# Idle TensorE multiplies constants before the second table and before the experts, and some register loads take bounds checks

## The reference

```python
x = x + gnn0(ln(x), src, dst, edge_weight, W, b)        # sum over 100000 edges of weighted rows, then @ W.T + b
x = x + ffn0(ln(x), wr, br, w1, b1, w2, b2)             # half of the rows chosen by a router, 256 -> 1024 -> 256
x = x + gnn1(ln(x), edge_weight1, weight, gate_weight, src, dst, edge_type_16)
#   all_msg = einsum('nf,rfo->rno', h, weight)          # 16 relations: the "second table"
#   msg = all_msg[rel, src] * norm * sigmoid(gate[rel, src]);  agg = segment_sum(msg, dst);  relu
x = x + ffn1(ln(x), Wg, bg, W1, b1, W2, b2)             # 8 experts, the top 2 of each row, 256 -> 1024 -> 256
```

## Time and profile before

| | |
|---|---|
| median of three executions | 4001.26 us (3999.29 to 4010.76) |
| span of the profiled execution, first to last instruction | 3402.6 us |
| median less span | 598.7 us |
| mean granted TensorE clock | 0.902 of full speed |
| TensorE busy | 2615.4 us, 77% of the span |
| GpSimd busy | 1869.7 us, 55% |
| VectorE busy | 1733.1 us, 51% |
| ScalarE busy | 723.6 us, 21% |

### The profile page before, as it was taken

One profiled execution on the slowest core, in us unless ns is written; L12 is line 12 of the kernel. 1 busy time (PEld: TensorE's weight loads), 2 busy tenths in 40 slices (PEclk: granted clock), 3 DMA queues, 4 the chain that ended last, 5 costly groups with the idle time before them and its releaser, 6 DMA issues. The chain is left out here.

```text
span 3402.6 us, 59974 instructions
## 1 busy us (share of the span) xinstructions
PE 2615.4 (77%) x14271; PEld 1921.6 (56%) x14272; DVE 1733.1 (51%) x5663; ACT 723.6 (21%) x1907; POOL 1869.7 (55%) x1915
## 2 busy tenths in 40 slices
PE   7688888887777799999655555564555389999997
PEld 6577777776665344444344444443444267767774
DVE  6455545454554655555355454544544544545553
ACT  4121111111110233333211010000000233333332
POOL 1777777777774000000377777777777245555554
PEclk9899999998999899999888888777777689999998
DMA  7333333333332444444545454555544623222232
GB/s 224 110 113 113 113 111 111 113 113 113 110 113 67 173 197 192 188 191 194 194 141 155 151 154 142 152 154 151 146 146 146 241 59 48 45 45 48 45 48 33
DMA packets 175589, 434.08 MB, mean 128 GB/s; under 512 B 41712, under 2 KB 103792, under 8 KB 169232
## 3 DMA queue, kind: packets, MB, share of 16 engines
q0 software_dynamic: 97072, 236.21, 26.9%
q1 hardware_dynamic: 57424, 183.78, 14.1%
q10 hardware_dynamic: 21008, 13.24, 1.3%
HBM read 275.05 MB, written 158.04 MB: 127 GB/s over the span
## 5 line engine op out<-in xcount | busy, mean ns | idle before, releaser
L776 POOL DMA_INDIRECT g_msg<-table,idx x1564 | 1517.3, 970 | 518.8 <-issue 476.5
L848 PE MATMUL psum<-g_msg,g_hot 128*128 x3328 | 967.4, 456 | 593.0 <-SPq L719 358.1
L848 PEld LDWEIGHTS psum<-g_msg,g_hot 128*128 128x128 f32 x3328 | 756.5, 233 | 789.5 <-issue 654.5
L796 DVE TENSOR_SCALAR g_hot<-iota,g_cols 128x128 f32<-128x128 f32 x1664 | 450.1, 364 | 31.9 <-DVE g_cols L793 30.5
L1908 POOL DMA_INDIRECT out<-ex_y,ex_to x112 | 206.0, 1839 | 253.9 <-DMA out<-ex_y,ex_to 165.3
L768 POOL MEMSET g_origin<- 128x256 f32 x1 | 0.3, 313 | 590.8 <-POOLq L1359 590.8
L1594 PE MATMUL psum<-wrel_halves,t_xhi 128*128 128x512 f16 x784 | 298.2, 380 | 1.7 <-DVE t_row L1475 1.7
L1595 PE MATMUL psum<-wrel_halves,t_xhi 128*128 128x512 f16 x784 | 298.1, 380 | 0.0
L1596 PE MATMUL psum<-wrel_halves,t_xlo 128*128 128x512 f16 x784 | 298.1, 380 | 0.0
L1475 DVE TENSOR_SCALAR t_row<-psum,t_gate 128x256 f32<-128x256 f32 x392 | 171.2, 479 | 233.7 <-PE psum L1596 231.7
L2074 PE MATMUL psum<-w,ex_ghi 128*128 x784 | 260.6, 382 | 6.7 <-DVE ex_y L1983 6.4
(11 more groups left out here) (353 smaller groups left out, 3231.7 us busy)
## 6 DMA issues: line engine op xcount, KB each, us to landing
table<-t_row SPq DMA_DIRECT2D x48, 2048.0 KB, 6.3
g_msg<-table,idx POOLq DMA_INDIRECT x1564
piece_stage<-in_w SPq DMA_DIRECT2D x32, 512.0 KB, 5.7
w_halves<-piece_halves SPq DMA_DIRECT2D x32, 512.0 KB, 3.4
w<-w_halves SPq DMA_DIRECT2D x8, 2048.0 KB, 22.6
rows<-sc_row ACTq DMA_DIRECT2D x50, 128.0 KB, 2.2
out<-acc ACTq DMA_DIRECT2D x49, 128.0 KB
table<-t_row SPq DMA_DIRECT2D x24, 256.0 KB, 2.5
```

Of the source, the lines that this page charges most:

```text
L776: pool.indirect_dma_start(out=msg[:, at:at + D], out_offset=None, in_=table, in_offset=bass.IndirectOffsetOnAxis(ap=t[f"idx{g}"][:, n:n + ...
L796: last = nc.vector.tensor_scalar(hot[b][:, k * P:(k + 1) * P], t["iota32"][:, :], c3[:, k, where:where + 1], c3[:, k, weight:weight + 1], ...
L848: pe.matmul(ps, hot[b % PAIR][:, k * P:(k + 1) * P], msg[:, bass.ds(slot_at[k], D)], start=False, stop=False, skip_group_check=True).then_ ...
```

## The change

Three edits.

1. In `table1`, TensorE's list gets ten matmuls of the identity by itself ahead of `turn(0, 0)` and three behind it, into bank 4, with no wait and no semaphore. Each is a 128x128 fp32 product.
2. In `experts`, behind the wait for the weights and ahead of `turn(0, 0)`, ten matmuls of a corner of `w1` by 512 of its columns (fp16) into bank 6.
3. In `gather`, `slot_number` and the load in `close_from` use `value_load`, so they make the bounds check; and the two thresholds that TensorE waits on in a batch are masked with 1023 first (three masks a batch).

```diff
+WARM_EXPERTS, WARM_TURN, WARM_LOGITS = 10, 10, 3
...
     def slot_number(eng, m):
-        _, (n,) = nc.values_load_multi_w_load_instructions(slot_at(m, 0, 1), engines=[eng.engine], min_val=0, max_val=WINDOWS,
-                                                           skip_runtime_bounds_check_because=sure)
-        return n
+        return eng.value_load(slot_at(m, 0, 1), min_val=0, max_val=WINDOWS)
...
-                    pe.wait_ge(tiles_in, code[MSG_TILES])
+                    pe.wait_ge(tiles_in, code[MSG_TILES] & 1023)
                     for k in range(BATCH):
                         if k % BANKS == 0:
-                            pe.wait_ge(bank_free, code[BATCH + k // BANKS] + 1)
+                            pe.wait_ge(bank_free, (code[BATCH + k // BANKS] & 1023) + 1)
...
                 with act.If(end - start >= k + 1):
-                    _, (n,) = nc.values_load_multi_w_load_instructions(
-                        t["closed"][0:1, bass.ds(m, 1)], engines=[act.engine], min_val=0, max_val=WINDOWS - 1 - k,
-                        skip_runtime_bounds_check_because=sure)
+                    n = act.value_load(t["closed"][0:1, bass.ds(m, 1)], min_val=0, max_val=WINDOWS - 1 - k)
                     close(n + k)
...
+            def warm(times):
+                for k in range(times):
+                    pe.matmul(psR[PAIRS % 4][:, 0:P], t["ident"][:, :], t["ident"][:, :], start=True, stop=True)
+
+            warm(WARM_TURN)
             turn(0, 0)
+            warm(WARM_LOGITS)
             logits(0, 0)
             pe.wait_ge(wrel_in, 16)
...
             pe.wait_ge(core.experts_in, 16 * core.experts_loads)
+            for k in range(WARM_EXPERTS):
+                pe.matmul(psY[0][:, :], w1[:, 0:P], w1[:, 0:2 * D], start=True, stop=True)
             turn(0, 0)
```

## The result

| | before | after |
|---|---|---|
| median | 4008.07 us (3996.53 to 4012.14, 9 runs) | 4042.38 us (4021.44 to 4061.29, 9 runs) |
| ratio after to before | | 1.0095, 95% interval 1.0076 to 1.0114 |
| profiled execution: its own time | not given | 4048.66 us |
| its span | 3402.6 us | 4046.9 us |
| mean granted clock | 0.902 | 0.816 |

The change costs 34.3 us, 0.9%, where I forecast no difference. The profiled execution of the changed kernel lasts 1.8 us longer than its span. So the 598.7 us that I had put around the span of the kernel before aren't there: its profile shows an execution of some 3404 us, and its timed executions took 600 us more. The comparison with its trace has to keep these two things apart.

What follows compares the result with a forecast made beforehand. GpSimd was taken to bound the gathers, TensorE the second table and, close beside GpSimd's adds, the experts. Terms of 2.3 + 1.4 - 0.5 = 3.2 us less than 4001.26 us gave 3998.1 us (ratio 0.9992), range 3992 to 4007.

Steps and rivals of the forecast that it cites:

- the 598.7 us around the span: Whole kernel: the 4001.26 us median taken as the profile's 3402.6 us span plus 598.7 us around it.
- Term 3: Gathers: checks and masks mostly hidden in TensorE's 3.9 us tile waits; 0.5 us lost, at each gather's end.
- The third rival: Gathers: queues lose the pace; if TensorE's queue paced, 104 turns would cost 22 to 40 us; chance 3%.
- Term 1: Start of second table: products raise the clock before the relations; 2.3 us less, bounds 0 and 2.7.
- My first rival: Clock falls again in the experts' pause, or never rises for identity products: 3999.1 or 4001.8 us; chance 35%.
- Term 2: Start of experts: ten products raise the clock; 1.4 us less, between 0.4 and 2.2.
- the two cases between which I had halved: Experts' start: clock holds through the pause, 2.2 us less, or falls in it, 0.4 us and a bit; even odds.

Runs made afterwards that it cites:

- case 2: Sessions in which the kernel before took 4000 us and over; no trace of that kernel exists there.
- after_again: The changed kernel run once more, against the kernel before at 4052.88 us: 4087.9 us, ratio 1.009.
- no_warm: The changed kernel without its 23 constant products, only checks and masks, against the kernel before at 4052.88 us: 4085.99 us, ratio 1.0097.
- masks_for_checks: no_warm with each added bounds check replaced by one mask, against the kernel before at 4052.88 us: 4076.98 us, ratio 1.0078.
- case 1: Sessions in which the kernel before took some 3400 us.
- pe_regs: no_warm with six more register operations a batch on TensorE, against the kernel before at 3401.19 us: 3424.95 us, ratio 1.0067.
- act_regs: no_warm with six more register operations a batch on ScalarE, against the kernel before at 3401.19 us: ratio 1.0004.
- lean: fold_one on top of masks_for_checks: two register operations a batch fewer on TensorE, masks for checks; ratio to the kernel before 0.9995.
- no_warm_2: no_warm run again, against the kernel before at 3401.32 us: 3401.14 us, ratio 1.0.
- section 5: The experiment with pe_regs12, which makes TensorE's queue the pace without slow stretches: ratio 1.0198 to the kernel before.
- after_3: The changed kernel run once more, against the kernel before at 3401.32 us: 3402.56 us, ratio 1.0003.
- both_half: The changed kernel with TensorE's and ScalarE's gather loop bodies halved, against the kernel before at 4052.88 us: 4135.66 us, ratio 1.0206.
- pe_regs12: no_warm with twelve more register operations a batch on TensorE, against the kernel before at 3406.59 us: 3474.66 us, ratio 1.0198.
- fold_one: no_warm with the +1 of the bank waits put into the table, two operations a batch fewer on TensorE; ratio to the kernel before 0.9999.

## Why the prediction was wrong

**The step that failed first: the 598.7 us around the span.** The sum was made against 3402.6 + 598.7 us, and all else was read as if the timed executions looked like the profile. They don't. Here an execution lasts 1.8 us longer than its span, of the kernel before as well (4057.15 and 4055.3 us in one). In the profiled execution GpSimd paced the gathers without a pause; in the timed ones the changed kernel shows slow stretches, and the kernel before, with 4008 us, can't have run as its trace shows. That its time of 4000 us is made of the same stretches is an inference from its time and its granted clock of 0.815 (the changed kernel: 0.816), since no trace of it in case 2 exists.

**The second, Term 3: "the per-batch ones lie in TensorE's 3.9 us of waiting for tiles".** Term 3 put the loss at 0.5 us; measured were 34.3. In case 2 that waiting is gone. TensorE waited for tiles 4 times, 29.3 us, in the changed kernel, none of it in gather 0, and GpSimd waited on the ring 99 times. With 0.081 us an operation, six masks and the two queue instructions of one check are eight operations a turn, 8 x 52 x 0.081 = 34 us in gather 0. Measured were 34.3, 35.0 and 33.1 us (result, after_again, no_warm). The check's two instructions show at TensorE's load of the slot's number: the trace of before has 108 TENSOR_LOAD and 104 FUSED_REGOPS there (line 685), that of the changed kernel 108 TENSOR_LOAD, 212 FUSED_REGOPS and 108 SEQ_ASSERT (line 686). For masks_for_checks, seven operations a turn, it gives 29 us, measured 24.1. The fit is close, but each of these differences is known to some 8 to 12 us only, the price comes from case 1, and no stage of the kernel before was seen in case 2. So that the loss lies in TensorE's queue in gather 0 is argued, not shown. Whether gather 1, where ScalarE has the stretches, adds to it stays open too: pe_regs, act_regs and lean, which would tell, all fell into case 1.

Even for case 1 the step was read from too coarse a row. 3.9 us was the mean of one wait over both gathers; over 104 turns the 358.1 us are 3.4 us a turn. Here is the kernel before in gather 0 alone (80 to 1118 us), then in gather 1 alone (1662 to 2732 us), then no_warm_2 in gather 0:

```profile
PE psum L848 <- SPq L719: 63.3, 25, 6.3
```
```profile
PE psum L848 <- SPq L719: 294.8, 67, 17.3
```
```profile
PE psum L846 <- SPq L717: 43.4, 16, 6.2
```

In gather 0, where TensorE also has the second tile's products, it waited 63.3 us in 52 turns, 1.2 us a turn and a third of what the step counted on. The change's eight operations, 0.65 us a turn (8 x 0.081), fit into that: behind them no_warm_2 still waits 0.8 us a turn, of which 0.5 could be filled (section 5). Hence 1.0003 in after_3.

**The third rival had the mechanism, as far as it is known, and the size, 22 to 40 us, and got 3%.** "If TensorE's queue were the pace" is what case 2 looks like in gather 0. It was dismissed because GpSimd never waited in the profile. The 18% by which the median exceeded the span should have kept it open. Its price of a mask, 32 ns, was the duration of the operation, not the distance to the next: 6 masks cost 0.49 us a turn, not 0.19. That its sum holds the measured 34 us is in part luck, since it multiplies this low price by the 104 turns of both gathers; at 0.081 us an operation both would give 68 us, and gather 0 alone 34.

**Term 1, the products before the second table, forecast 2.3 us.** It came true in two traces of four. That a 128-column fp32 product is two passes is plain in the changed kernel's trace, where the thirteen products are 26 records, as the eight products of a batch are sixteen in the earlier trace rows:

```profile
L1628 PE MATMUL psum<-ident x26: 275/421/554, 1593.2 to 1598.7; 128*128 128x128 f32 x26
```

The first ten products, 20 records, lasted 4.61 us there and 4.22 in after_3, against 4.0 in the sum, which held so far. In the result's own trace the clock rose 5.2 us behind the end of the gather's block and held, the relations ran at a pitch of 0.22 us from the first one, and the second tile's transposes came 13.4 us behind the block's end, with a short wait for `t_xn`, instead of 15.6 in the kernel before (TensorE of the changed kernel, at the first logits, the first relations and the second tile):

```profile
1600.28 0.17 PE L1591 MATMUL psum<-wgate_hi,t_xhi 128*128 128x16 f16 x1 [1.25 <-DVE t_xlo L1456]
...
1600.43 0.38 PE L1591 MATMUL psum<-wrel_halves,t_xhi 128*128 128x512 f16 x1
...
1606.13 0.41 PE L1583 MATMUL psum<-ident,t_xn 128*128 128x128 f32 x2 [0.37 <-DVE t_xn L209]
```

after_again is like it (13.5 us). In after_3 and both_half the clock fell again. Busy time by stretch of after_3, from 0.9 us ahead of the end of the gather's block on, then of no_warm_2, from 3.8 us behind it on:

```profile
1116.00:1120.00 4.00, 2.52 (x12) 2.55 (x13) 2.56 (x16) 0.00 (x0) 0.00 (x0) 0.50 1.07 341
1120.00:1124.00 4.00, 2.78 (x18) 2.43 (x17) 3.39 (x15) 0.38 (x1) 0.00 (x0) 0.86 0.09 30
1124.00:1128.00 4.00, 3.48 (x14) 1.35 (x15) 3.34 (x16) 1.94 (x4) 0.00 (x0) 0.57 0.03 6
1128.00:1132.00 4.00, 4.00 (x21) 2.00 (x20) 2.71 (x13) 1.23 (x5) 0.00 (x0) 1.00 0.00 0
```
```profile
1122.00:1126.00 4.00, 0.87 (x9) 0.53 (x10) 3.53 (x12) 0.38 (x1) 0.00 (x0) 0.50 0.01 4
1126.00:1130.00 4.00, 4.00 (x14) 1.41 (x12) 3.20 (x19) 2.30 (x4) 0.00 (x0) 0.50 0.00 0
1130.00:1134.00 4.00, 4.00 (x20) 1.92 (x19) 2.12 (x9) 1.11 (x3) 0.00 (x0) 0.97 0.00 0
```

The clock of after_3 rose early, to 0.86 between 1120 and 1124. Then it fell again about the first relations, and the first eight of them ran at the lower clock (TensorE of after_3, at the first logits, the first relation, the first fast ones and the second tile):

```profile
1124.52 0.17 PE L1591 MATMUL psum<-wgate_hi,t_xhi 128*128 128x16 f16 x1 [1.25 <-DVE t_xlo L1456]
...
1124.68 0.59 PE L1591 MATMUL psum<-wrel_halves,t_xhi 128*128 128x512 f16 x1
...
1128.24 0.38 PE L1591 MATMUL psum<-wrel_halves,t_xhi 128*128 128x512 f16 x1
...
1131.48 0.38 PE L1583 MATMUL psum<-ident,t_xn 128*128 128x128 f32 x2
```

Here the second tile's transposes came at 14.6 us, as in both_half. The pause ahead of the logits is 1.25 us both in the result's trace, where the clock held, and in after_3, where it fell, so the pause alone doesn't decide it; why the two differ is not shown. In the sixteen traces without the products, whose programs are alike at this place, the transposes came at 14.6 to 15.6 us, 15.1 in the mean, and the kernel before is at the late end. So from run to run the rise moves by as much as half of the term. The second table lasted 540.2 and 540.5 us where the clock held, 541.6 and 541.4 where it fell, and 542.2 in the mean without the products (541.4 to 543.0). The term is worth some 1.8 us in the one case and some 0.7 in the other, and bounded as the prediction said, by 0 and 2.7. My first rival, a clock that falls again, happens in `table1` as well, against which I had named the three products behind the transposes.

**Term 2, before the experts, forecast 1.4 us.** The products ran and the clock was up for the first `up` products in all four traces that have them: in after_3 these lie 0.11 us apart from 2740.14 on, in no_warm_2 0.21 us. TensorE won some 2 us by it: the 24th of them starts 9.8 us behind the block's end there and 12.0 in no_warm_2. That is the better of the two cases between which I had halved. The first output add of GpSimd came 31.1 us behind the block's end instead of 33.2 (32.1 in the kernel before). But the experts lasted 669.8 us against 669.3 (668.2 to 671.6 in the case 1 traces without the products). What ends this stage are GpSimd's adds, which wait for each other's transfers: these are 12% of the span in the chain that ended last, on the pages of both. Their waits in after_3, then in no_warm_2:

```profile
POOL out L1911 <- DMA out<-ex_y,ex_to: 163.7, 54, 3.2
...
POOL out L1911 <- DVE ex_y L1986: 13.2, 1, 13.2
```
```profile
POOL out L1904 <- DMA out<-ex_y,ex_to: 163.7, 54, 3.2
...
POOL out L1904 <- DVE ex_y L1979: 23.2, 3, 18.0
```

GpSimd waited 10 us less for rows of `y` and the stage was no shorter. That the adds took the 2 us back is read from these rows; no run changed the adds. I had named this chain as close beside TensorE and then costed the stage by TensorE alone. Both terms together: after_3 and no_warm_2 differ by 1.4 us in the wrong direction, less than the 0.09% of their intervals, so what the products are worth in the time is not resolved.

## What to carry to other kernels

Put the profile's span beside the times before anything else: if they differ by much more than an execution differs from its own span (here 598.7 us against 1.8), the profile is of another kind of execution than the times, and every "hidden behind" read from it holds for that kind alone. Spare time of an engine is read for each stage by itself (1.2 us a turn in gather 0, where the mean over both gathers was 3.4), and an instruction queue's price by what more of its operations cost (0.081 us each here) or by the distance between starts (0.095 us), not by durations (0.032 us). Products that only raise the clock may work in one execution and not in the next (before the second table in two traces of four), so one trace doesn't tell their worth, and the stage has to end on that engine.

## What the runs showed of the hardware

- The same program takes 3400 or 4000 us and more, within 1% of itself in a session. The kernel before took 4008 and 4053 us in two sessions and 3401 to 3407 us in four. One chip number, 6, stands by both 4053 and 3407 us, so by the record the chip alone doesn't decide it. In the changed kernel the difference comes with slow stretches of TensorE in gather 0 (10.5 us in the mean) and of ScalarE in gather 1 (13.3 us), with starts at multiples of 0.70 us. One execution of fold_one took 6484.03 us at a clock of 1.00, has no trace, and is in no ratio.
- In gather 0 they come mostly once in a turn of some 207 recorded instructions of TensorE, at about the same place, and whether a loop body holds one turn (both_half) or two doesn't matter. The traces of case 1 have no stretch on TensorE. That in case 2 TensorE waits for its instructions is my guess, and the recorded fetches don't bear it out. This row of the DMA queue that fetches instructions (packets, MB, share of time) is the same in the changed kernel's trace of case 2 and in after_3:

```profile
q14 instruction: 68, 0.56, 0.0%
```

  Both traces have 22 such packets of 8 KB and more in gather 0 and 21 in gather 1, and of the 43 stretches of TensorE in gather 0 only 3 have one inside or within 1 us ahead. No run here shows the cause: the pace of the gathers' transfers and the place of the program in memory were not told apart.
- A register operation costs 0.081 us of the time of TensorE's queue once that queue is the pace (pe_regs12), with a recorded duration of 0.032 us.
- No version beat the kernel before in case 1 (lean: 0.9995, 0.9992, 0.9998). lean was not run in case 2, where it has three operations a turn more than the kernel before on TensorE instead of eight. By 0.081 us it should lose 13 instead of 34 us; that is an estimate.
